# Pre-norm attention with a low-rank expert layer: two tiles first in the prologue, some tiles normalised on GpSimd, the layer's bias on TensorE

## The chip, the cores and the metric

The kernel runs on one core of one Trainium2 chip. The metric is the device time of one execution in microseconds (us). Engines by the names of the profile: PE is TensorE (PEld its weight loads), DVE VectorE, ACT ScalarE, POOL GpSimd, SP SyncE, which here only issues DMAs; SPq and ACTq are the queues of DMA-issuing instructions.

## The reference

x is 8 x 256 x 128 in float32. First attention over 16 heads of 64 is added to x, then a linear layer with eight low-rank experts.

```python
x = x + attention(layernorm(x))
x = x + ffn(layernorm(x))
# attention, for each batch and head:
scores = q @ k.T * 64**-0.5 + einsum('id,ijd->ij', q, rel_k[clip(i - j, -64, 64) + 64])
scores = where(scores < 32nd largest of the row, -inf, scores)
attn = softmax(scores)
a1 = attn @ v + einsum('ij,ijd->id', attn, rel_v[...]); a2 = attn @ a1; a3 = attn @ a2
out = (al0 * a1 + al1 * a2 + al2 * a3) @ Wout.T + bout
# ffn:
y = x @ base_w.T + base_b
gate = softmax(x @ router_w.T + router_b)            # 8 experts
y = y + 2 * sum over e of gate[e] * (x @ lora_A) @ lora_B[e]
```

## The kernel before

x lies as 16 tiles of 128 rows, two (T = 2) for each batch. The heads are worked off in pairs: 8 batches by 8 pairs (NP) are 64 pairs, 128 heads g. Each engine runs its own list of instructions, and semaphores tie them. The lists are written as slots q = -3 to 67, a software pipeline over the pairs: in slot q TensorE makes queries and keys of pair q+3 (`queries_and_keys`), the product with the relative keys of pair q+2 (`relative_keys`) and the scores of pair q+1 (`scores`); VectorE finds the top 32 of heads 2q and 2q+1 (`top`, four rounds of MAX8 with MATCH_REPLACE8 between them); ScalarE and GpSimd turn them into the softmax one head behind.

The relative term needs a shift of each row by its number. ScalarE copies the product out (`save_band`), GpSimd fills its edges (`fill_band`), SyncE writes it to a scratch in HBM (band_scratch) and reads it back at a slant (skew), and GpSimd adds it to the scores (`add_skew`, which releases `top`). The scratch has zeros written to it once.

For head g the way from the top values to the softmax is: `scale_limit` (GpSimd, after the last MAX8 of g), `ramp` (ScalarE, "pen"), `add_penalty` (GpSimd), `exponent` (ScalarE), and the reciprocal of its sum on VectorE in `divide(g)`, which stands at the end of `top(g+1)`. So an exponent that comes late holds VectorE there.

SyncE's order in the prologue is: x and the weights `wqkv`, the zeros of the scratch, eight small loads, then the slots; after slot -1 `load_wout` (wout, bout and the zeros of a second scratch, diag_scratch), after slot 0 `load_ffn`. `wqkv` has one block of 192 KB for each of the eight pairs of a batch. Its parts have semaphores: w_in for blocks 0 and 1, w_in2 for 2 to 7. TensorE waits for w_in2 in `queries_and_keys(2)`, ahead of slot 0.

The second norm and the layer (`layer`, 144 columns: 128 of the layer, 8 of the router, 8 of lora_A) run in the loop for the first six batches (INSIDE), one batch in eight slots, and save to ffn without bias. In the tail VectorE adds the bias to 12 tiles (`add_bias`, twice six), and GpSimd adds ffn onto the residual (`add_base`), whose tile is named x_sb in the profile. Four pairs' outputs are mixed on VectorE in the tail (`mix_part`) and projected on TensorE (`project_mix`).

Of the kernel before, what the change touches and what calls it, by code (L numbers as in the profile page):

```python
# [6 lines left out]
def preln_attention_ffn(nc: bass.Bass, x_d, wqkv_d, bqkv_d, wout_d, bout_d, relk_d, relv_d, relvc_d, alphas_d,  # L7
# [43 lines left out]
    with ctx:  # L51
# [1254 lines left out]
```

## Time and profile before

| | us |
|---|---|
| median of 3 runs (lowest, highest) | 702.81 (702.47, 704.76) |
| the profiled execution, its own time | 702.51 |
| its span in the profile | 700.8 |
| VectorE busy | 682.2 (97%) |
| TensorE busy | 651.9 (93%) |
| ScalarE busy | 619.5 (88%) |
| GpSimd busy | 549.4 (78%) |
| share of the chain that ended last: VectorE, TensorE, GpSimd | 76%, 11%, 3% |

The profiled execution lies 0.30 us under the median, inside the spread of the runs. Span and own time differ by 1.7 us, which lie around the profiled instructions. The busy shares are means over three stages: a prologue up to the first MAX8, a loop of 128 heads, and a tail behind the last one.

### The profile page before, as it was taken

The numbers are of one execution on the slowest core, as the hardware profiler recorded it, in microseconds if no ns is written. First come the engines' busy times: TensorE is split into PE (matmuls) and PEld (weight loads), VectorE is DVE, ScalarE is ACT, GpSimd is POOL, SyncE is SP. The second block draws the span as 40 slices with busy tenths as digits, with TensorE's granted clock in tenths as the row PEclk, the third lists the DMA queues.
The fourth block names the chain that finished last, engine by engine and source line by source line (L and its number), as shares of the span: only waits on it lengthen the run. The fifth ranks groups of instructions, "written<-read, shape, count | busy, mean of one in ns | idle before, by whom it ended". The sixth has DMA issues, their size and how long they took to land.

```text
span 700.8 us, 20904 instructions
## 1 busy us (share of the span) xinstructions
PE 651.9 (93%) x5748; PEld 505.8 (72%) x5748; DVE 682.2 (97%) x2827; ACT 619.5 (88%) x1772; POOL 549.4 (78%) x985
## 2 busy tenths in 40 slices
PE   5388999999999999999999999999999999998896
PEld 3266777777777777777787777877777777777664
DVE  6899999999999999999999999999999999999995
ACT  4589998999999999999999999998999999998763
POOL 1589898888878888878887888788887888877760
PEclk9789999999999999999999999999999999999998
DMA  6854454545455544545454545444454545445322
GB/s 200 184 146 146 140 153 127 164 131 161 125 154 140 154 136 135 152 130 167 131 159 126 153 139 145 147 151 140 131 154 135 164 133 154 129 130 162 87 58 61
DMA packets 148338, 98.72 MB, mean 141 GB/s; under 512 B 10624, under 2 KB 147968, under 8 KB 148096
## 3 DMA queue, kind: packets, MB, share of 16 engines
q1 hardware_dynamic: 147920, 97.32, 48.1%
q8 instruction: 48, 0.79, 0.5%
q14 instruction: 66, 0.54, 0.3%
q10 hardware_dynamic: 304, 0.08, 0.1%
HBM read 45.59 MB, written 51.77 MB: 139 GB/s over the span
## 4 chain that ended last, share of the span: by engine, by line
DVE 76%; PE 11%; issue 5%; POOL 3%; DMA 2%; ACT 2%; DVEq 1%; SPq 1%; ACTq 0%; POOLq 0%
DVE top L790 37%; DVE work L796 36%; PE ps_p L1053 2%; DMA band_scratch<-zeros 1%; PE ps_y L1073 1%; DVE rinv L777 1%; POOL s_sb L347 1%; PE ps_a L961 1%; PE ps_s L1010 1%; ACT a_sb L505 1%; PE ps_d L1030 1%; POOL a_sb L352 1%; PE ps_p L999 1%; DVEq L185 1%; POOL s_sb L322 1%
## 5 line engine op out<-in xcount | busy, mean ns | idle before, releaser
L790 DVE MAX8 top<-work 128x8 f32<-128x256 f32 x768 | 286.0, 415 | 0.0
L796 DVE MATCH_REPLACE8 work<-top,work 128x256 f32<-128x256 f32 x512 | 205.9, 410 | 0.0
L347 POOL TENSOR_TENSOR s_sb<-s_sb,pen 128x512 f32<-128x512 f32 x127 | 162.0, 1275 | 25.6 <-ACT pen L495 20.1
L505 ACT ACTIVATE a_sb<-s_sb,nmax 128x256 f32<-128x256 f32 x254 | 127.3, 502 | 23.1 <-POOL s_sb L347 14.6
L322 POOL TENSOR_TENSOR s_sb<-s_sb,skew 128x384 f32<-128x384 f32 x128 | 128.3, 1003 | 2.9 <-DMA skew<-band_scratch 2.9
L495 ACT ACTIVATE pen<-s_sb,limit 128x256 f32<-128x256 f32 x254 | 116.4, 512 | 12.6 <-POOL limit L334 12.3
L1053 PE MATMUL ps_p<-aT,rows 128*64 128x256 f32 x1024 | 125.3, 386 | 1.8 <-ACT rows L585 1.0
L352 POOL TENSOR_SCALAR a_sb<-a_sb,rinv 128x256 f32<-128x256 f32 x254 | 118.8, 478 | 1.6 <-DVE rinv L777 1.5
L796 DVE MATCH_REPLACE8 work<-top,s_sb 128x256 f32<-128x256 f32 x256 | 102.9, 410 | 0.0
L1053 PEld LDWEIGHTS ps_p<-aT,rows 128*64 128x64 f32 x1024 | 67.6, 136 | 40.5 <-issue 10.4
L790 DVE MAX8 top<-s_sb 128x8 f32<-128x256 f32 x256 | 94.1, 410 | 2.1 <-POOL s_sb L322 2.1
L961 PE MATMUL ps_a<-ident,a_sb 128*128 128x128 f32 x512 | 84.8, 289 | 12.2 <-POOL a_sb L352 12.2
L334 POOL TENSOR_SCALAR limit<-top 128x2 f32<-128x2 f32 x127 | 24.3, 192 | 81.0 <-DVE top L790 80.7
L961 PEld LDWEIGHTS ps_a<-ident,a_sb 128*128 128x128 f32 x512 | 54.5, 142 | 43.5 <-issue 28.8
L488 ACT COPY aT<-ps_a 128x512 f32<-128x512 f32 x128 | 72.3, 565 | 1.2 <-PE ps_a L961 1.2
L543 ACT COPY s_sb<-ps_s 128x512 f32<-128x512 f32 x128 | 68.9, 595 | 0.3 <-PE ps_s L1010 0.2
L1030 PE MATMUL ps_d<-aT,v_sb 128*64 128x256 f32 x504 | 65.4, 381 | 2.5 <-ACT diagT L548 2.5
L1010 PE MATMUL ps_s<-k_sb,q_sb 64*128 64x256 f32 x512 | 66.2, 377 | 0.0
L975 PE MATMUL ps_qk<-xnT,wqkv 128*128 128x256 f32 x128 | 43.8, 425 | 10.2 <-ACT v_sb L553 8.2
L1030 PEld LDWEIGHTS ps_d<-aT,v_sb 128*64 128x64 f32 x504 | 35.4, 137 | 21.8 <-ACT diagT L548 4.7
L999 PEld LDWEIGHTS ps_p<-relkt,q_sb 64*128 64x128 f32 x512 | 34.2, 190 | 22.7 <-issue 22.7
L361 POOL TENSOR_TENSOR clip<-aT,mask 128x256 f32<-128x256 f32 x64 | 47.9, 748 | 3.3 <-ACT aT L488 3.3
(176 smaller groups left out, 1331.8 us busy)
## 6 DMA issues: line engine op xcount, KB each, us to landing
skew<-band_scratch SPq DMA_DIRECT2D x128, 192.0 KB, 2.8
diag_scratch<-a_sb SPq DMA_DIRECT2D x128, 192.0 KB, 3.1
band_scratch<-band SPq DMA_DIRECT2D x128, 191.0 KB, 3.7
diag<-diag_scratch SPq DMA_DIRECT2D x128, 128.0 KB, 2.2
wqkv<-in_wqkv SPq DMA_DIRECT2D x1, 1152.0 KB, 8.0
x_sb<-in_x SPq DMA_DIRECT2D x4, 256.0 KB, 4.9
wout<-in_wout SPq DMA_DIRECT2D x1, 512.0 KB, 6.1
out<-xn SPq DMA_DIRECT2D x1, 512.0 KB, 3.2
```

The source lines that it names most:

```text
L322: nc.gpsimd.tensor_tensor(near, near, skew[p % 2][:, g % 2, :, :], ALU.add).then_inc(s_added, 1)
L347: nc.gpsimd.tensor_tensor(s_sb[g % 4][:], s_sb[g % 4][:], pen[g % 2][:], ALU.subtract).then_inc(pen_added, 1)
L352: nc.gpsimd.tensor_scalar(a_sb[g % 3][:, t, :], a_sb[g % 3][:, t, :], rinv[g % 2][:, t:t + 1], 1.0, ALU.mult, ALU.mult).then_inc(normed, 1)
L488: nc.scalar.copy(aT[p % 4][:, g % 2, :, :].rearrange("p c n -> p (c n)"), ps_a[:]).then_inc(t_saved, 1)
L495: nc.scalar.activation(pen[g % 2][:, t, :], s_sb[g % 4][:, t, :], ACT.Relu, bias=limit[g % 2][:, t:t + 1], scale=-STEEP).then_inc(ramp_don ...
L505: nc.scalar.activation(a_sb[g % 3][:, t, :], s_sb[g % 4][:, t, :], ACT.Exp, bias=nmax[g % 2][:, t:t + 1], scale=1.0, accum_out=rsum[g % 2] ...
L790: nc.vector.max(m[:, t, 8 * n:8 * n + 8], src).then_inc(top_step, 1)
L796: nc.vector.match_replace(work[t][:, n % 2, :], m[:, t, 8 * n:8 * n + 8], src, LOW).then_inc(top_step, 1)
L961: last = transpose(ps_a[:, c * N + t * P:c * N + (t + 1) * P], a_sb[g % 3][:, t, c * P:(c + 1) * P], ident[:])
L1010: last = mm(ps_s[h][:, t * N:(t + 1) * N], q_sb[p % 3][d, t * P:(t + 1) * P], k_sb[p % 3][d, :], start=True, stop=True)
L1030: mm(r1[d, 0:N], v_sb[p % 2][:, c, d], aT[p % 4][:, h, c, :], start=(c == 0), stop=False)
L1053: last = mm(ps[d, 0:N], r[:, i, c, d], aT[p % 4][:, h, c, :], start=(c == 0), stop=(c == T - 1))
```

## The change

In the prologue two tiles of x (one batch) and one block of weights come first, then the zeros, then the rest of x, and the eight small loads are one (`late`, laid out on the host). The remaining weights go in three parts: block 1 (w_in), blocks 2 and 3 (w_in2), issued inside slot -1, and blocks 4 to 7 (w_in3), issued after slot -1. TensorE multiplies `ones` by itself 11 times (WARM) before it has work. VectorE takes the moments and the norm of two tiles first; of the other 14 it normalises 8, GpSimd 6 (tiles 10 to 13 in slot -1, 14 and 15 in slot 0). The columns of xn go to TensorE in five groups (2, 4, 4, 4, 2 tiles) in place of four. ScalarE takes the second root after the copies of pairs 0 and 1. In the loop `layer` begins with a product of the identity and the bias, and GpSimd's `add_base` runs for two tiles at the end of slots 19, 27, ... 59. In the tail VectorE's two `add_bias` and GpSimd's two additions over six tiles are gone.

```diff
 @block.sync
-            for g in range(GROUPS):
-                sp.dma_start(x_sb[:, 4 * g:4 * g + 4, :], x_d[2 * g:2 * g + 2].rearrange("b (t p) d -> p (b t) d", p=P)
-                             ).then_inc(x_in[g], 16)
-                if g == 0:
-                    sp.dma_start(wqkv[:, 0:2, :], wqkv_d[:, 0:2 * 3 * P].rearrange("p (h c) -> p h c", h=2)).then_inc(w_in, 16)
-            sp.dma_start(wqkv[:, 2:NP, :], wqkv_d[:, 2 * 3 * P:].rearrange("p (h c) -> p h c", h=NP - 2)).then_inc(w_in2, 16)
-            sp.wait_ge(made, MADE)
+            load_x(0, 1, x_first)
+            load_weights(0, 1, w_first)
+            sp.wait_ge(made, 2)
             for i in range(2):
                 dst = bass.AP(band_d[i].tensor, DYN, [[2 * ROW, P], [ROW, 2], [1, P]])
                 sp.dma_start(dst, zeros[:, 0:2 * P].rearrange("p (h c) -> p h c", h=2)).then_inc(scratch_zero, 16)
-            for dst, src in ((relvc[0:DH, :], relvc_d), (relvc[DH:P, :], relvc_d),
...
-                sp.dma_start(dst, src).then_inc(late_in, 16)
+            load_x(1, 2, x_in[0])
+            load_weights(1, 2, w_in)
+            for g in range(1, GROUPS):
+                load_x(2 * g, 2 * g + 2, x_in[g])
+            sp.dma_start(late[:], late_d).then_inc(late_in, 16)
...
+                if q == -1:
+                    load_weights(2, 4, w_in2)
...
                 if q == -1:
+                    load_weights(4, NP, w_in3)
                     load_wout()
 @block.gpsimd
+            def normal_rows(a, e):
+                pool.wait_ge(rstd_done, 2)
+                for i in range(a, e):
+                    nc.gpsimd.tensor_scalar(xn[:, i, :], x_sb[:, i, :], mv[:, i, 0:1], rstd[:, i:i + 1], ALU.subtract,
+                                            ALU.mult).then_inc(xn_aside, 1)
...
+                if b >= 1 and q % NP == 3:
+                    pool.wait_ge(layer_saved, T * b)
+                    add_base(T * (b - 1), T * b)
...
-            for i, (a, e) in enumerate(((0, T * INSIDE // 2), (T * INSIDE // 2, T * INSIDE), (T * INSIDE, DONE))):
-                pool.wait_ge(f_saved, i + 1)
-                add_base(a, e)
+            pool.wait_ge(f_saved, 1)
+            add_base(T * INSIDE, DONE)
 @block.scalar
             save_queries(0)
+            save_band(0)
+            save_scores(0)
+            save_queries(1)
+            save_band(1)
             act.wait_ge(var_done, 2)
-            nc.scalar.activation(std[:, 4:TILES], mv[:, 4:TILES, 1], ACT.Sqrt).then_inc(std_done, 1)
-            save_band(0)
+            nc.scalar.activation(std[:, T:TILES], mv[:, T:TILES, 1], ACT.Sqrt).then_inc(std_done, 1)
             act.wait_ge(made, MADE)
             nc.scalar.activation(warm[:, 0:1], warm[:, 0:1], ACT.Exp).then_inc(warmed, 1)
-            save_queries(1)
-            save_band(1)
-            save_scores(0)
-            act.wait_ge(late_in, 16 * 8)
+            act.wait_ge(late_in, 16)
 @block.vector
-            moments(0, 4)
+            moments(0, T)
             dve.wait_ge(std_done, 1)
-            normal_rows(0, 4)
+            normal_rows(1, 0, T, T)
...
-            add_bias(0, T * INSIDE // 2)
-            add_bias(T * INSIDE // 2, T * INSIDE)
+            dve.wait_ge(layer_saved, T * INSIDE)
             add_layer_bias(T * INSIDE, DONE)
 @block.tensor
-                mm(ps_p1[:, N:N + FFN], ynT[:, i * P:(i + 1) * P], wffn[:], start=True, stop=True).then_inc(layer_ready, 1)
+                mm(ps_p1[:, N:N + FFN], ident[:], bffn[:], start=True, stop=False)
+                mm(ps_p1[:, N:N + FFN], ynT[:, i * P:(i + 1) * P], wffn[:], start=False, stop=True).then_inc(layer_ready, 1)
...
+            pe.wait_ge(made, 2)
+            for _ in range(WARM):
+                mm(ps_d[:, 0:P], ones[:], ones[:], start=True, stop=True)
             pe.wait_ge(made, MADE)
             normal_columns(0)
             queries_and_keys(0)
-            for q in (-2, -1):
-                relative_keys(q + 2)
-                if on(q + 1):
-                    scores(q + 1)
-                queries_and_keys(q + 3)
+            relative_keys(0)
+            scores(0)
+            queries_and_keys(1)
+            relative_keys(1)
+            queries_and_keys(2)
```


SyncE's order, from the first write of the scratch to the reads of pair 1 (band is the write of the scratch, skew the read; the waits name semaphores). Before:

```order
L280 DMA band_scratch<-band 128x2x191 [waits band_filled,scratch_zero]
L280 DMA band_scratch<-band 128x2x191 [waits band_filled]
L264 DMA skew<-band_scratch 128x2x192 [waits band_out0]
L264 DMA skew<-band_scratch 128x2x192 [waits band_out1]
L280 DMA band_scratch<-band 128x2x191 [waits band_filled] x2
L230 DMA wout<-in_wout 128x8x128
L230 DMA bout<-in_bout 128x128
L233 DMA diag_scratch<-zeros 128x2x64 x4
L264 DMA skew<-band_scratch 128x2x192 [waits band_out2]
L264 DMA skew<-band_scratch 128x2x192 [waits band_out3]
```

And now:

```order
L289 DMA band_scratch<-band 128x2x191 [waits band_filled,scratch_zero]
L289 DMA band_scratch<-band 128x2x191 [waits band_filled]
L271 DMA skew<-band_scratch 128x2x192 [waits band_out0]
L271 DMA skew<-band_scratch 128x2x192 [waits band_out1]
L219 DMA wqkv<-in_wqkv 128x768
L289 DMA band_scratch<-band 128x2x191 [waits band_filled] x2
L219 DMA wqkv<-in_wqkv 128x1536
L237 DMA wout<-in_wout 128x8x128
L237 DMA bout<-in_bout 128x128
L240 DMA diag_scratch<-zeros 128x2x64 x4
L271 DMA skew<-band_scratch 128x2x192 [waits band_out2]
L271 DMA skew<-band_scratch 128x2x192 [waits band_out3]
```

Weights of blocks 2 and 3 (128x768) and of 4 to 7 (128x1536) moved from ahead of the zeros, above this piece, to behind the first reads of the scratch, the first ahead of the write for pair 1, the second behind it.

TensorE's order from the relative keys of pair 1 to those of pair 2 (L975 and L978, now L1000 and L1003, are queries and keys; L999, now L1024, the relative keys; L1010 the scores). Before:

```order
L999 MATMUL ps_p<-relkt,q_sb 128x128 [waits band_saved,qk_saved,relk_done]
L999 MATMUL ps_p<-relkt,q_sb 128x128 x3
L1010 MATMUL ps_s<-k_sb,q_sb 128x256 [waits qk_saved]
L1010 MATMUL ps_s<-k_sb,q_sb 128x256 x3
L975 MATMUL ps_qk<-xnT,wqkv 128x256 [waits qk_saved,w_in2,xnT_saved]
L978 MATMUL ps_qk<-xnT,wqkv 128x256
L975 MATMUL ps_qk<-xnT,wqkv 128x256 [waits qk_saved,xnT_saved,relv_done]
L978 MATMUL ps_qk<-xnT,wqkv 128x256
L999 MATMUL ps_p<-relkt,q_sb 128x128 [waits band_saved,qk_saved,relk_done]
L999 MATMUL ps_p<-relkt,q_sb 128x128 x3
```

And now:

```order
L1024 MATMUL ps_p<-relkt,q_sb 128x128 [waits band_saved,qk_saved,relk_done]
L1024 MATMUL ps_p<-relkt,q_sb 128x128 x3
L1000 MATMUL ps_qk<-xnT,wqkv 128x256 [waits qk_saved,w_in2,xnT_saved]
L1003 MATMUL ps_qk<-xnT,wqkv 128x256
L1000 MATMUL ps_qk<-xnT,wqkv 128x256 [waits qk_saved,xnT_saved,relv_done]
L1003 MATMUL ps_qk<-xnT,wqkv 128x256
L1024 MATMUL ps_p<-relkt,q_sb 128x128 [waits band_saved,qk_saved,relk_done]
L1024 MATMUL ps_p<-relkt,q_sb 128x128 x3
```

The scores of pair 0, which stood behind the relative keys of pair 1, moved ahead of the queries of pair 1; the wait on w_in2 stands where it did, between pair 1 and all that follows.

GpSimd's order around the first heads (L332 is `add_skew`, L337 the norm, L343 `negative_max`, L359 `fill_band`, L350 `scale_limit`, L363 `add_penalty`), now:

```order
L337 TENSOR_SCALAR xn<-x_sb,mv,rstd 128x128 [waits rstd_done]
L337 TENSOR_SCALAR xn<-x_sb,mv,rstd 128x128 x3
L332 TENSOR_TENSOR s_sb<-s_sb,skew 128x2x192 [waits s_saved,skew_in0]
L343 TENSOR_SCALAR nmax<-top_0 128x2 [waits top_step]
L332 TENSOR_TENSOR s_sb<-s_sb,skew 128x2x192 [waits s_saved,skew_in1]
L337 TENSOR_SCALAR xn<-x_sb,mv,rstd 128x128 [waits rstd_done]
L337 TENSOR_SCALAR xn<-x_sb,mv,rstd 128x128
L359 TENSOR_SCALAR band<-band 128x2x2x63 [waits band_saved]
L350 TENSOR_SCALAR limit<-top_0 128x2 [waits top_step]
L343 TENSOR_SCALAR nmax<-top_1 128x2 [waits top_step]
L363 TENSOR_TENSOR s_sb<-s_sb,pen 128x512 [waits ramp_done]
L332 TENSOR_TENSOR s_sb<-s_sb,skew 128x2x192 [waits s_saved,skew_in2]
```

The two stretches of L337 are new, and the fill of pair 2's band stood ahead of the second `add_skew` before.

## Rows read from the trace of the kernel before

**Rows 1.** Windows of the prologue, the loop and the tail: busy us and instructions of each engine.

```profile
20.10:671.00 650.90, 619.69 (x5515) 483.42 (x5512) 649.56 (x2716) 597.61 (x1722) 537.69 (x961) 0.99 0.50 143
```

**Rows 2.** Chain that ended last, in order of time: start us, us, what.

```profile
4.63 9.11 DMA band_scratch<-zeros
...
13.76 2.77 DMA band_scratch<-band
...
20.14 0.74 DVE top L790 x2
...
30.25 0.64 DVE top L790 x2
```

**Rows 3.** Timeline of the prologue: start us, us, engine, line, op, tiles, count.

```profile
0.92 0.53 POOL L301 MEMSET zeros<- 128x512 f32 x1
...
7.08 1.09 PE L953 MATMUL ps_y<-ident,xn 128*128 128x128 f32 x4 [7.08 <-DVE xn L752]
...
8.84 1.22 PE L975 MATMUL ps_qk<-xnT,wqkv 128*128 128x256 f32 x2 [0.67 <-ACT xnT L482]
...
10.85 1.23 PE L999 MATMUL ps_p<-relkt,q_sb 64*128 64x128 f32 x8
...
12.92 0.44 POOL L343 TENSOR_SCALAR band<-band 128x252 f32<-128x252 f32 x1 [9.79 <-ACT band L537]
...
19.42 0.72 PE L999 MATMUL ps_p<-relkt,q_sb 64*128 64x128 f32 x8
...
19.97 1.03 PE L1010 MATMUL ps_s<-k_sb,q_sb 64*128 64x256 f32 x8
```

**Rows 4.** Timeline of TensorE from 39 us on.

```profile
39.08 1.10 PE L975 MATMUL ps_qk<-xnT,wqkv 128*128 128x256 f32 x2
39.98 1.06 PE L978 MATMUL ps_qk<-xnT,wqkv 128*128 128x256 f32 x2
```

**Rows 5.** Windows of TensorE after 27 us: busy us, granted clock, DMA share, GB/s.

```profile
27.00:28.00 1.00, 0.00 (x0) 0.86 1.11 367
28.00:29.00 1.00, 0.00 (x0) 0.50 1.08 315
```

**Rows 6.** Windows of the prologue, all engines: the last figure is GB/s.

```profile
9.00:10.00 1.00, 1.00 (x3) 0.82 (x4) 1.00 (x9) 0.00 (x0) 0.00 (x0) 1.00 0.98 404
```

**Rows 7.** Timeline of SyncE, 18 to 19 us.

```profile
18.09 0.36 SPq L264 DMA_DIRECT2D skew<-band_scratch  x1
18.49 0.47 SPq L280 DMA_DIRECT2D band_scratch<-band  x1
```

**Rows 8.** DMA issues: KB each, median us to landing.

```profile
wqkv<-in_wqkv SPq DMA_DIRECT2D x1, 384.0 KB, 4.1
```

**Rows 9.** Timeline, 21 to 29 us, ScalarE and GpSimd.

```profile
21.03 1.07 ACT L543 COPY s_sb<-ps_s 128x512 f32<-128x512 f32 x2
...
25.52 0.91 ACT L495 ACTIVATE pen<-s_sb,limit 128x256 f32<-128x256 f32 x2 [3.42 <-POOL limit L334]
...
28.18 1.00 POOL L322 TENSOR_TENSOR s_sb<-s_sb,skew 128x384 f32<-128x384 f32 x1 [0.40 <-DMA skew<-band_scratch]
...
28.72 0.19 ACT L505 ACTIVATION_READ_ACCUMULATOR a_sb<-s_sb,nmax 128x1 f32 x1
```

**Rows 10.** Timeline of the tail.

```profile
674.27 1.92 DVE L836 TENSOR_TENSOR ffn<-ffn,bffn 128x816 f32<-128x816 f32 x2
...
676.74 4.36 POOL L443 TENSOR_TENSOR x_sb<-x_sb,ffn 128x768 f32<-128x768 f32 x3
...
676.89 1.79 DVE L848 TENSOR_TENSOR gate<-ffn,lmax 128x112 f32<-128x112 f32 x1
...
681.96 0.71 PE L1081 MATMUL ps_y<-wout,mix 128*128 128x128 f32 x4 [0.43 <-DVE mix L864]
```

**Rows 11.** Timeline of GpSimd in slot 27.

```profile
303.70 0.19 POOL L334 TENSOR_SCALAR limit<-top 128x2 f32<-128x2 f32 x1 [1.40 <-DVE top L790]
```

**Rows 12.** Groups of GpSimd's instructions: count, busy us, mean ns.

```profile
L410 POOL TENSOR_TENSOR x_sb<-x_sb,yp_sb 128x256 f32<-128x256 f32 x7 | 5.1, 730 | 0.0
```

More of the change, by code:

```diff
@@ L31, in preln_attention_ffn @@
     T = N // P
+    ORDER = (late_d.shape[1] - T - 2 * T * DH) // NP
     TILES = B * T
@@ L203, in preln_attention_ffn @@
         DONE = TILES - T
+        WARM = 11
+        ASIDE = DONE - 4
         GROUPS = TILES // 4
+        COLUMNS = [(0, T)] + [(a, min(a + 4, TILES)) for a in range(T, TILES, 4)]
         MIXED = PAIRS - len(mix)
@@ L747, in moments, with normal_rows @@
                 nc.vector.tensor_scalar(mv[:, a:e, 1], mv[:, a:e, 1], EPS, None, ALU.add).then_inc(var_done, 1)
[L749 to L751 removed]
+            def normal_rows(n, a, e, last):
+                nc.vector.reciprocal(rstd[:, a:e], std[:, a:e]).then_inc(rstd_done, 1)
+                dve.wait_ge(rstd_done, n)
+                for i in range(a, last):
                     nc.vector.tensor_scalar(xn[:, i, :], x_sb[:, i, :], mv[:, i, 0:1], rstd[:, i:i + 1],
                                             ALU.subtract, ALU.mult).then_inc(xn_done, 1)
[L755 removed]
+            moments(0, T)
             dve.wait_ge(std_done, 1)
[L757 to L758 removed]
+            normal_rows(1, 0, T, T)
+            dve.wait_ge(relk_in, 16)
             own(nc.vector.tensor_scalar(relkt[:, 0, :], relk[:, 0:P], relk[:, P:VOCAB], None, ALU.subtract))
@@ L890, in _ @@
             dve.wait_ge(alpha_exp, 1)
-            own(nc.vector.tensor_scalar(al[:], al[:], 1.0, None, ALU.add))
-            nc.vector.reciprocal(al[:], al[:]).then_inc(alpha_done, 1)
+            own(nc.vector.tensor_scalar(al, al, 1.0, None, ALU.add))
+            nc.vector.reciprocal(al, al).then_inc(alpha_done, 1)
             for g in range(HEADS):
@@ L949, in normal_columns @@
             def normal_columns(g):
-                pe.wait_ge(xn_done, 4 * (g + 1))
+                a, e = COLUMNS[g]
+                if e <= ASIDE:
+                    pe.wait_ge(xn_done, e)
+                else:
+                    pe.wait_ge(xn_aside, e - ASIDE)
                 reach(pe, xnT_saved, g)
-                for i in range(4):
-                    last = transpose(ps_y[:, i * P:(i + 1) * P], xn[:, 4 * g + i, :], ident[:])
+                for i in range(a, e):
+                    last = transpose(ps_y[:, (i - a) * P:(i - a + 1) * P], xn[:, i, :], ident[:])
                 last.then_inc(xnT_ready, 1)
```

94 lines of the change are left out of this document (49 added, 45 removed).

## The prediction

> **What bounds the kernel now.** I read the windows by stage first. From 20.1 to 671 us VectorE works 649.56 of 650.90 us [rows 1]: the loop is its own bound, and 1.3 us is all that any rearrangement inside it could win. So the change can pay at two places, before the loop and behind it, and only by what reaches VectorE. The chain in order of time shows the first: the zeros of the scratch land at 13.74 us, pair 0's band is written (issued 13.76), read back and added, and the first MAX8 runs at 20.14 us; 10.11 us later, at 30.25 us, head 2 begins [rows 2]. From the issue of the band to the first MAX8 it is 6.38 us. In the prologue's timeline TensorE starts at 7.08 us and the band's edges are filled by 12.92 + 0.44 = 13.36 us [rows 3], 0.4 us before the zeros have landed. So before, two chains end together there: the zeros, queued behind all weights, and the computation.
>
> **The early prologue.** TensorE's first products are slow: queries 1.22 us and relative keys 1.23 us, where the same shape takes 0.72 us at 19.42 us [rows 3]. The windows show the clock go from 0.86 to 0.50 of the full 2.4 GHz by 28 us, after TensorE had been idle since 24 us [rows 5], and with 0.50 granted the queries take 1.10 us [rows 4]; so I read the prologue's first products as running at 1.2 GHz too. The products of ones can start when GpSimd's zeros are made, 0.92 + 0.53 = 1.45 us [rows 3]. One of 256 columns follows another by 39.98 - 39.08 = 0.90 us at the low clock [rows 4], so one of 128 by 0.45 us, and 11 end at 6.4 us, a little earlier if the clock rises among them; I take 6.2 us. Two normalised tiles are there before that (my estimate is 5.4 us), so TensorE begins 0.9 us earlier than before, and at the high clock. From 7.08 to 13.36 us lie 6.28 us. Half the transposes at twice the rate save 0.7 of 1.09 us, the queries 0.6 of 1.22, the relative keys 0.51 of 1.23 [rows 3], a copy of half the columns some 0.2: 2.0 us. The band is filled at 6.2 + 6.28 - 2.0 = 10.5 us and issued at once, since the zeros now have less data ahead of them; if the clock stays low, it is 11.5 us. The first MAX8 comes at 10.5 + 6.4 = 16.9 us, 3.2 us earlier.
>
> On the Trainium skill's page "SBUF — State Buffer", section "Who interferes with whom", VectorE and GpSimd share a port pair that one holds for a whole instruction. By that rule the 8 norms of VectorE and the 4 of GpSimd in slot -1 would stand in each other's way, and top(0) would come at some 17.3 in place of 16.9 us. The trace agrees in the tail, where a VectorE instruction over 112 elements takes 1.79 us beside GpSimd's long addition [rows 10]. As the next part has it, neither figure is the one that counts.
>
> **What is late next.** Head 2 can't begin before its skewed scores are added and before VectorE has passed `divide(0)` at the end of top(1), which needs exponent(0). Both get later relative to the start.
>
> Weights of blocks 2 and 3 are issued behind the read of pair 0's second head, and that read waits for its own write: before, it was issued at 18.09 us [rows 7], 4.33 us after the band. The next issue stood at 18.49 us [rows 7], 4.73 us after the band. So they are issued at 10.5 + 4.7 = 15.2 us. 384 KB took 4.1 us to land behind x [rows 8]; with less ahead I take 3.2 us, the ends being 2.8 and 4.1: landed at 18.4 us (18.0 to 19.3). Up to then TensorE can do nothing behind the relative keys of pair 1, which end near 12.3 us. That is 6 us of idleness; before, 4 us sufficed for the clock to drop [rows 5]. I therefore cost what follows at the low clock: queries and keys of pair 2 to 18.4 + 1.96 (39.08 to 41.04) [rows 4], the keys' copy and its wait 0.65, pair 3's queries and keys 1.8, relative keys of pair 2 1.16, and scores twice the 1.03 us of [rows 3] less their overlap, 1.9: 7.5 us. The last copy of the scores adds 0.6 (a half of 1.07) [rows 9]: 26.5 us. Only then does ScalarE come to ramp(0), since it stands behind these copies. From ramp to the end of exponent it took 25.52 to 28.91, 3.4 us [rows 9], and the reciprocal 0.2: head 2 begins at 18.4 + 11.7 = 30.1 us against 30.25 us. Before, ScalarE had done the scores by 22.10 us and waited 3.42 us for the limit [rows 9]; that reserve pays for the shift. **The 3.2 us won at head 0 come down to 0.15 us at head 2.**
>
> The page "TensorE: Matmul & The Clock Gate", section "Part 1: The HAM clock gate", of the Trainium skill says that the throttled clock is the default and only activity lifts it. By that rule the 11 products of ones buy speed for the first pair and lose it again in this wait.
>
> **The other limit of head 2** is the DMA queue. Before, from the issue of pair 1's band at 18.49 us [rows 7] to the landing of its skew at 28.18 us [rows 9] it was 9.7 us with the DMA engines nearly full, its share over 1 near the end [rows 5]. Now this begins at 15.7 us and has 1152 KB of weights in it, which at 404 GB/s [rows 6] are 2.9 us: landed at 28.3 us, or 27.8 us if some fill the gaps; plus 1.0 us of addition [rows 9], head 2 at 28.8 to 29.3 us. At the high clock this one decides, otherwise the 30.1 us.
>
> **The loop.** 12 products of 144 columns are added on TensorE, some 0.25 us each, far from the heads that VectorE needs next: nothing. GpSimd gets six additions of 128x256 at 0.73 us (L410 is the same shape) [rows 12], at a slot's end, where in slot 27 it waited 1.40 us for the next limit [rows 11]: hidden. Behind them stand `scale_limit` and the softmax chain; without that cover each costs 0.73 us, 4.4 us together. The six norms on GpSimd (estimate: under 0.5 us each) stand ahead of additions that have a whole head's time.
>
> **The tail.** VectorE loses 1.92 us of bias additions, GpSimd most of its 4.36 us, beside which VectorE's 1.79 us would shrink to some 0.3 [rows 10]. VectorE gains over 4 us there. But it is not the bound: TensorE waited 0.43 us for the mix at 681.96 us [rows 10], and otherwise works through its own chain of powers with ScalarE, to which the last residual is tied. Gain 0.45 us; floor 0, and if the mixes had been on the path throughout, 2 us.
>
> **Sum.** 0.15 + 0.45 = 0.6 us off the profiled execution's 702.51 us: 701.9 us. That execution lies 0.3 us below the median of the runs, 702.81 us, from which it would be 702.2 us. Since the errors I know of (clock, packing of DMAs) mostly shorten, I put it at 701.8 us.
>
> **Rivals.**
> 1. *The queue decides* (the clock is up when the weights land, or rises soon): head 2 at 28.8 to 29.3, so 0.95 to 1.45 plus 0.45: 700.6 to 701.1 us. For it: the idle stretch is cut short if the weights land early. Against it: idleness beyond that of [rows 5].
> 2. *The whole gain arrives:* VectorE runs through from 16.9, head 2 at 27.0, 3.25 + 0.45 = 3.7 us: 698.8 us. It wants weights by some 18 us, a high clock, and a queue 2 us faster than I cost it. For it: the zeros and small loads no longer delay anything.
> 3. *Slower: the second part of the weights.* Head 2 begins 11.7 us after they land. The edge is 19.0 us: with the tail's gain, landing later than that loses. At 20 us head 2 begins at 31.7: 1.45 lost, 0.45 won, 703.5 us; more than 0.3% slower takes a landing after 21.1 us, as would come with the band at 11.5 us and a landing time far over the 4.1 us of [rows 8].
>
> **How the numbers follow.** A measurement here tells about 0.3%, 2.1 us. Forecast 0.55 (its own range 700.6 to 703.1, from the ends of the landing and of the clock in the prologue), rival 1 0.2, rival 2 0.13, rival 3 0.12. Faster by over 2.1 us: all of rival 2, the lower end of rival 1 and a little of the forecast, 0.24. Slower: half of rival 3, 0.06. Same: 0.70. The range is 698.8 to 703.4 us: it takes in rival 2's value and half of rival 3.
>
> **What would show it.** Right: the first MAX8 near 17 us, TensorE idle from 12.3 to 18.4 us, its queries of pair 2 over 1 us long, VectorE waiting 2 to 3 us for exponent(0) or for the skew ahead of head 2, head 2 near 30 us; no new waits of VectorE in the loop; at the tail's mixes no wait of TensorE, and the last MAX8 to the end 0.45 us shorter. Wrong: no wait ahead of head 2 (rival 2), or a stall at slots 19 to 59, which would say that GpSimd's additions delay the limit.

## The result, and the profile of the changed kernel

Over 22 runs each in turn, the kernel before took 703.27 us (median; 700.91 to 705.97) and the changed one 704.65 us (702.48 to 708.74): a ratio of 1.0023 with a 95% interval of 1.0012 to 1.0033. The change costs 1.6 us by this ratio (1.4 us between the two medians). That is less than the 0.3% named in the prediction, but the interval excludes no change, and 704.65 us lies above the predicted range. The profiled execution took 706.07 us, its span 704.3 us (before 702.51 and 700.8).

The timeline of the prologue of the changed kernel, all engines:

```profile
1.51 5.06 PE L1217 MATMUL ps_d<-ones 128*128 128x128 f32 x22 [1.51 <-POOL zeros L311]
...
7.46 0.70 PE L1000 MATMUL ps_qk<-xnT,wqkv 128*128 128x256 f32 x2 [0.46 <-ACT xnT L506]
...
8.88 0.71 PE L1024 MATMUL ps_p<-relkt,q_sb 64*128 64x128 f32 x8 [0.29 <-ACT q_sb L549]
...
10.90 0.88 SPq L289 DMA_DIRECT2D band_scratch<-band  x2
...
14.28 3.28 POOL L337 TENSOR_SCALAR xn<-x_sb,mv,rstd 128x128 f32<-128x128 f32 x4
...
15.02 0.47 SPq L219 DMA_DIRECT2D wqkv<-in_wqkv  x1
...
17.53 0.99 POOL L332 TENSOR_TENSOR s_sb<-s_sb,skew 128x384 f32<-128x384 f32 x1
...
18.55 0.75 DVE L817 MAX8 top<-s_sb 128x8 f32<-128x256 f32 x2 [1.61 <-POOL s_sb L332]
...
20.50 1.19 PE L1000 MATMUL ps_qk<-xnT,wqkv 128*128 128x256 f32 x2 [7.65 <-issue]
...
28.18 1.07 ACT L567 COPY s_sb<-ps_s 128x512 f32<-128x512 f32 x2 [0.67 <-PE ps_s L1035]
...
29.14 0.92 ACT L519 ACTIVATE pen<-s_sb,limit 128x256 f32<-128x256 f32 x2
...
32.56 0.17 DVE L804 RECIPROCAL rinv<-rsum 128x2 f32<-128x2 f32 x1 [3.96 <-ACT a_sb L529]
32.67 0.75 DVE L817 MAX8 top<-s_sb 128x8 f32<-128x256 f32 x2
```

Read from the top: the products of ones end at 6.6 us, and the queries and relative keys of pair 0 take 0.70 and 0.71 us in place of the 1.22 and 1.23 of [rows 3]. Pair 0's band is issued at 10.90 us, 2.9 us earlier than in [rows 2]. At 18.55 the first MAX8 runs, 1.6 us earlier. But TensorE idles for 7.65 us until the weights of blocks 2 and 3 are there, ScalarE comes to the mask of head 0 (`pen`) only behind copies of scores that TensorE makes after that wait, and VectorE, done with head 1, waits 3.96 us. Its MAX8 at 32.67 us is head 2, which stood at 30.25 us in [rows 2]. The 1.6 us won at head 0 are 2.4 us lost at head 2.

The DMA issues of the weights, with KB and us from issue to landing, answer to [rows 8]:

```profile
wqkv<-in_wqkv SPq DMA_DIRECT2D x1, 768.0 KB, 7.8
...
wqkv<-in_wqkv SPq DMA_DIRECT2D x1, 384.0 KB, 5.4
```

15.02 + 5.4 = 20.4 us: the product at 20.50 us starts as they land. TensorE's windows (busy us, granted clock, DMA share, GB/s) show what the idle stretch does to the clock, as [rows 5] did before:

```profile
12.00:13.00 1.00, 0.72 (x8) 1.00 1.01 318
13.00:14.00 1.00, 0.00 (x0) 1.00 0.05 14
14.00:15.00 1.00, 0.00 (x0) 0.51 0.32 39
```

TensorE works 0.72 us in the first of these windows and then stands still; in the one from 14 us on the grant is 0.51, that is, it falls from 2.4 to 1.2 GHz, and the queries at 20.50 us take 1.19 us.

The window of the loop, from the MAX8 of head 2 to the last mask, has the columns of [rows 1]:

```profile
32.60:675.20 642.60, 617.57 (x5507) 483.08 (x5508) 640.36 (x2676) 594.70 (x1712) 537.72 (x958) 0.99 0.49 142
```

VectorE idles 2.2 us in it, 0.9 us more than before. Most of that are two waits, at 276.41 us (0.33) and 288.22 us (1.44), each 6 us behind a late diagonal on TensorE. One of these in the timeline:

```profile
270.69 0.63 PE L1046 MATMUL ps_d<-ident,diag 128*128 128x128 f32 x4 [1.67 <-issue]
...
276.41 0.17 DVE L804 RECIPROCAL rinv<-rsum 128x2 f32<-128x2 f32 x1 [0.33 <-ACT a_sb L529]
```

GpSimd's six additions, 0.73 to 0.74 us each, lie in slots where it waits for VectorE anyway. The tail, beside [rows 10]:

```profile
679.43 0.46 DVE L862 TENSOR_TENSOR ffn<-ps_s,bffn 128x288 f32<-128x288 f32 x1 [0.80 <-PE ps_s L1243]
...
680.18 0.73 POOL L428 TENSOR_TENSOR x_sb<-x_sb,ffn 128x256 f32<-128x256 f32 x1
680.23 0.82 DVE L868 TENSOR_TENSOR gate<-ffn,lmax 128x112 f32<-128x112 f32 x1
...
684.53 0.48 DVE L884 SCALAR_TENSOR_TENSOR mix<-r3T,late,mix 128x256 f32<-128x256 f32 x1 [2.70 <-ACT r3T L595]
```

The bias additions of 1.92 us are gone, GpSimd has one addition in place of three, and the gate takes 0.82 us in place of 1.79. VectorE now waits 2.70 us for ScalarE. From the last mask (670.73 us before, 675.01 after) to the start of VectorE's last addition it is 27.30 us before and 26.62 after: 0.68 us won.

**The books of the two profiles.** Head 2 +2.5 us (the timeline has before's at 30.16 us, from where the chain of [rows 2] follows on at 30.25), loop +1.8 us (from 640.6 to 642.3), tail -0.7 us: +3.6 us, against spans that differ by 3.5 us. All runs together give 1.6 us only, which is about head 2 and the tail alone (+1.8). So either the loop's 1.8 us belong to the profiled execution, or the profiles mislead. The experiments had to settle that, and what head 2 waits for.

### The profile page after: what moved, and what is told of

Read it like the earlier page. It is cut to its first block, busy times and chain, and to the rows that moved or that the text cites. A ratio compares the mean times of both kernels' runs of the same rounds, so it can differ in the third digit from the quotient of the medians.

```text
span 704.3 us, 20995 instructions
## 1 busy us (share of the span) xinstructions
PE 658.7 (94%) x5794; PEld 513.0 (73%) x5794; DVE 677.0 (96%) x2819; ACT 620.6 (88%) x1773; POOL 554.3 (79%) x995
## 4 chain that ended last, share of the span: by engine, by line
DVE 64%; PE 24%; issue 4%; POOL 2%; ACT 1%; DVEq 1%; ACTq 0%; POOLq 0%
DVE top L817 32%; DVE work L823 31%; PE ps_p L1078 5%; PE ps_y L1098 3%; PE ps_a L984 2%; PE ps_d L1055 2%; PE ps_s L1035 2%; PE ps_p L1024 1%; PE ps_qk L1000 1%; PE ps_d L1046 1%; PE ps_qk L1011 1%; PE ps_d L1063 1%; PE ps_d L1128 1%; PE ps_qk L1003 1%; POOL s_sb L363 1%
## 5 line engine op out<-in xcount | busy, mean ns | idle before, releaser
L363 POOL TENSOR_TENSOR s_sb<-s_sb,pen 128x512 f32<-128x512 f32 x127 | 161.9, 1275 | 35.3 <-ACT pen L519 30.7
L332 POOL TENSOR_TENSOR s_sb<-s_sb,skew 128x384 f32<-128x384 f32 x128 | 128.4, 1003 | 0.0
L984 PEld LDWEIGHTS ps_a<-ident,a_sb 128*128 128x128 f32 x512 | 54.1, 141 | 39.7 <-issue 28.8
L350 POOL TENSOR_SCALAR limit<-top 128x2 f32<-128x2 f32 x127 | 24.3, 191 | 66.2 <-DVE top L817 66.1
L1000 PE MATMUL ps_qk<-xnT,wqkv 128*128 128x256 f32 x128 | 42.9, 418 | 16.0 <-issue 7.7
L1024 PEld LDWEIGHTS ps_p<-relkt,q_sb 64*128 64x128 f32 x512 | 34.4, 190 | 22.7 <-issue 22.7
```

What stands on the lines that cost most here:

```text
L332: nc.gpsimd.tensor_tensor(near, near, skew[p % 2][:, g % 2, :, :], ALU.add).then_inc(s_added, 1)
L363: nc.gpsimd.tensor_tensor(s_sb[g % 4][:], s_sb[g % 4][:], pen[g % 2][:], ALU.subtract).then_inc(pen_added, 1)
L984: last = transpose(ps_a[:, c * N + t * P:c * N + (t + 1) * P], a_sb[g % 3][:, t, c * P:(c + 1) * P], ident[:])
```

## The experiments

All numbers of one kernel in one table. "Loop" is from head 2's first MAX8 to the last mask, "tail" from there to VectorE's last addition, in us, all from one profile; the ratio is to the kernel before in the same comparison. e1 to e4, e5 to e9, e10 to e13, and e14 with e15 were each compared on one chip; across these groups the ratios are less sure than within.

| kernel | first MAX8 | head 2 | loop | tail | ratio (95%) |
|---|---|---|---|---|---|
| before | 20.14 | 30.16 | 640.57 | 27.30 | 1 |
| changed | 18.55 | 32.67 | 642.34 | 26.62 | 1.0023 (1.0012 to 1.0033) |
| e1 loop and tail only | 20.62 | 30.64 | 640.91 | 26.76 | 0.9985 (0.9974 to 0.9996) |
| e2 prologue only | 18.59 | 32.13 | 641.52 | 27.31 | 1.0015 (1.0001 to 1.0029) |
| e3 weights early | 18.57 | 28.62 | 641.97 | 26.30 | 0.9981 (0.9968 to 0.9994) |
| e4 all weights early | 19.29 | 29.31 | 642.05 | 26.86 | 0.9984 (0.9970 to 0.9998) |
| e5 norms behind skew | 17.86 | 28.94 | 640.25 | 26.31 | 0.9986 (0.9972 to 0.9999) |
| e7 no ones | 18.89 | 28.91 | 639.97 | 26.76 | 0.9973 (0.9962 to 0.9984) |
| e8 one load | 18.81 | 34.94 | 640.56 | 26.32 | 1.0067 (1.0042 to 1.0092) |
| e9 wout later | 17.66 | 27.68 | 640.81 | 26.76 | 0.9976 (0.9964 to 0.9989) |
| e10 e9, no ones | 18.33 | 28.36 | 641.17 | 26.75 | 0.9948 (0.9927 to 0.9969) |
| e11 e9, norms on VectorE | 19.39 | 29.35 | 641.57 | 26.31 | 0.9969 (0.9948 to 0.9989) |
| e12 changed again | 18.39 | 32.84 | 640.83 | 26.75 | 1.0036 (1.0009 to 1.0063) |
| e13 before again | 19.89 | 29.92 | 642.42 | 27.33 | 0.9982 (0.9954 to 1.0010) |
| e14 weights alone | 18.47 | 31.96 | 643.12 | 26.63 | 1.0020 (1.0000 to 1.0041) |
| e15 blocks 4 to 7 later | 18.54 | 32.01 | 642.73 | 26.32 | 1.0005 (0.9984 to 1.0026) |

**The two halves of the change.** e1 has the prologue of before and the edits of loop and tail:

```diff
-                mm(ps_p1[:, N:N + FFN], ynT[...], wffn[:], start=True, stop=True).then_inc(layer_ready, 1)
+                mm(ps_p1[:, N:N + FFN], ident[:], bffn[:], start=True, stop=False)
+                mm(ps_p1[:, N:N + FFN], ynT[...], wffn[:], start=False, stop=True).then_inc(layer_ready, 1)
...
+                if b >= 1 and q % NP == 3:
+                    pool.wait_ge(layer_saved, T * b)
+                    add_base(T * (b - 1), T * b)
```

> The prologue of before with the change's loop and tail alone. Theory (the late weights of pairs 2 and 3 cost the time, the loop edits are hidden and the tail gains 0.7 us): 0.1% faster than before, about 702.6 us, head 2 near 30.2 us, no new wait of VectorE in the loop. Rival (the bias on TensorE or GpSimd's additions bring the stalls seen in the loop of the changed kernel, 1.8 us near 280 us): 0.1 to 0.3% slower than before, with waits of VectorE for the exponent between 200 and 660 us.

Measured: ratio 0.9985, 1.1 us faster, interval 0.3 to 1.8. In the loop VectorE waits twice, 0.3 us each, and the tail is 0.54 us shorter than before's. e2 is the reverse, the new prologue with loop and tail of before.

> The change's prologue with the loop and tail of before. Theory: slower than before by what head 2 is late (2.4 us in the profile) and a little more, 0.3 to 0.4%, about 705.5 us. Rival (the loop edits cost the time): equal to before or faster.

Measured: ratio 1.0015, 1.1 us slower; half of what was expected; VectorE waits 3.38 us ahead of head 2, at 32.13 us. So the loss is in the prologue, and the rest of the change is a gain. The size of each is less sure: the two halves add up to nothing, where the whole change costs 1.6 us, and the three intervals together allow for about 1.5 us. e1 also shows how far an unaltered prologue moves by itself: its head 2 comes at 30.64 us, in the two profiles of the kernel before at 30.16 and 29.92.

**What head 2 waits for.** e3 is the changed kernel with one line moved: blocks 2 and 3 are loaded behind `late` and no longer behind the skew read of pair 0.

```diff
             sp.dma_start(late[:], late_d).then_inc(late_in, 16)
+            load_weights(2, 4, w_in2)
...
-                if q == -1:
-                    load_weights(2, 4, w_in2)
```

> The changed kernel with the weights of pairs 2 and 3 issued right behind the load of the small tensors, ahead of the waits of the slots. Theory: TensorE's 7.7 us wait ahead of the queries of pair 2 goes, head 2 begins one run of top(0) and top(1) after the first MAX8, at 28.7 us in place of 32.7 us, and the time falls by 4 us to about 700.7 us, 0.35% under before. Rival (the DMA queue holds the skew of pair 1 anyway): head 2 at 30 us or later, 702 us.

The timeline of e3 (TensorE, SyncE, GpSimd, VectorE):

```profile
12.87 0.70 PE L999 MATMUL ps_qk<-xnT,wqkv 128*128 128x256 f32 x2
...
16.58 0.44 SPq L238 DMA_DIRECT2D wout<-in_wout  x1
...
18.16 5.10 SPq L241 DMA_DIRECT2D diag_scratch<-zeros  x4
...
23.30 0.98 SPq L272 DMA_DIRECT2D skew<-band_scratch  x2
...
27.59 1.00 POOL L331 TENSOR_TENSOR s_sb<-s_sb,skew 128x384 f32<-128x384 f32 x1 [1.38 <-DMA skew<-band_scratch]
...
28.62 0.76 DVE L816 MAX8 top<-s_sb 128x8 f32<-128x256 f32 x2
```

TensorE has pair 2's weights at 12.87 us, VectorE's wait of 3.96 us is gone, and head 2 begins at 28.62 us, 4.05 us earlier than in the changed kernel. The time is now below that of before (0.9981, where 0.35% less was expected). One line turns the loss into a gain. The row at 27.59 shows the next limit: the skew of pair 1 lands only 1 us ahead of head 2.

e4 loads blocks 4 to 7 there as well (`load_weights(4, NP, w_in3)` behind the line above).

> As e3_w2_early, and the weights of pairs 4 to 7 behind them, so all weights are ahead of pair 0's band in the queue. Theory: the band waits for 1152 KB more, nearly 3 us, the first MAX8 comes at 19.5 to 20.5 us, and the time is 702 us. Rival (what queues behind the band does the harm, not what stands ahead): as fast as e3_w2_early or faster, near 700.5 us.

The additional 768 KB delay the skew of pair 0 (first MAX8 19.29), head 2 comes at 29.31, and the time is that of e3 within the intervals, not the 702 us of the theory (median 700.92).

e8 goes the other way and doubles the suspected cost: blocks 2 to 7 in one load at the changed kernel's place.

```diff
                 if q == -1:
-                    load_weights(2, 4, w_in2)
+                    load_weights(2, NP, w_in2)
...
-                    load_weights(4, NP, w_in3)
```

> The changed kernel, with the weights of blocks 2 to 7 in one load at the place where it loads blocks 2 and 3 (issued near 15.0 us). A doubling of the suspected cost. Theory (head 2 begins 12.2 us after these weights have landed): 1152 KB took 8.0 us before, so they land near 23.0 us in place of 20.4 and head 2 begins near 35.2 in place of 32.7, time 2.5 us above the changed kernel (ratio to before about 1.006). Rival (what delays the changed kernel against e3 is something else, for instance the second skew read or the traffic as a whole): head 2 within 0.5 us of 32.7 and no change in time, ratio 1.002.

```profile
23.17 1.19 PE L997 MATMUL ps_qk<-xnT,wqkv 128*128 128x256 f32 x2 [10.91 <-issue]
...
34.83 0.17 DVE L803 RECIPROCAL rinv<-rsum 128x2 f32<-128x2 f32 x1 [5.96 <-ACT a_sb L528]
```

The weights land 2.7 us later than in the changed kernel, and head 2 begins 2.3 us later, 11.8 us behind them (12.2 in the changed kernel); the ratio is 1.0067 (six runs), 4.7 us over before. The theory's 35.2 us was met within 0.3 us. That head 2 follows the landing of these weights is shown in both directions, and so is that the time follows head 2, if not us for us: e3 moves head 2 by 4.05 us and the ratio by 0.42%, 3.0 us.

**Why the landing took 5.4 us.** e14 issues everything that stood behind the 384 KB (blocks 4 to 7, wout, bout, zeros) behind the skew read of pair 1; e15 moves blocks 4 to 7 alone.

```diff
                         sp.dma_start(skew[p % 2][:, h, :, :], src).then_inc(skew_in[(2 * p + h) % 4], 16)
+                if q == 0:
+                    load_weights(4, NP, w_in3)
+                    load_wout()
...
-                if q == -1:
-                    load_weights(4, NP, w_in3)
-                    load_wout()
```

> The changed kernel with all that it issues behind the weights of blocks 2 and 3 (768 KB of weights at 16.52 us, wout, bout, the zeros of the diagonals) issued behind the read of pair 1's skew instead. In the changed kernel the 384 KB issued at 15.02 us landed at 20.4, 5.4 us later; before the change they took 4.1. Theory A (what is issued behind them shares the DMA engines and delays them): landed in 3.2 to 4.1 us, near 18.2 to 19.1 us, first product of pair 2 there, head 2 11.8 to 12.2 us later at 30.2 to 31.2 us, time 1.5 to 2.4 us below the changed kernel (ratio to before 1.000). Rival B (the reads and writes of the bands ahead of and beside them delay them): still 5.0 to 5.6 us, landing at 20.2 or later, head 2 above 32 us, no change against the changed kernel.

> The changed kernel with only the 768 KB of weights of blocks 4 to 7 moved behind the read of pair 1's skew; wout's 512 KB follow blocks 2 and 3 directly. Theory A by volume (anything large behind them delays them): 5 us or more as in the changed kernel, head 2 near 32.5. Theory A2 (the weights of blocks 4 to 7 in particular): as in e14. Rival B: as the changed kernel in both.

The row of these weights in e14, first, and in a second block in e15:

```profile
wqkv<-in_wqkv SPq DMA_DIRECT2D x1, 384.0 KB, 4.2
```

```profile
wqkv<-in_wqkv SPq DMA_DIRECT2D x1, 384.0 KB, 5.2
```

With only pair 1's band issued closely behind them they take 4.2 us, with wout's 512 KB behind them too 5.2, and in three profiles of the changed prologue 5.4, 5.4 (e2) and 6.0 us (e12). That fits theory A, which would put some 1.2 us down to the large loads behind, and the bands' traffic alone doesn't give 5 us, against rival B. But it is one profile each, and the kernel before speaks against it. This is its order of issue, and then the row of its 384 KB in e1, which has the same prologue:

```profile
0.79 0.45 SPq L210 DMA_DIRECT2D x_sb<-in_x  x1
...
1.30 0.49 SPq L213 DMA_DIRECT2D wqkv<-in_wqkv  x1
...
1.84 1.52 SPq L210 DMA_DIRECT2D x_sb<-in_x  x3
...
3.40 0.51 SPq L214 DMA_DIRECT2D wqkv<-in_wqkv  x1
```

```profile
wqkv<-in_wqkv SPq DMA_DIRECT2D x1, 384.0 KB, 5.6
```

There the 384 KB (blocks 0 and 1) have 768 KB of x and 1152 KB of weights issued behind them within 2.1 us, more than in the changed kernel, and landed in 4.1 us in both profiles of before, but in 5.6 us in e1. So one and the same place gives landings 1.5 us apart, more than the 1.2 us in question, and how much the loads behind cost stays open. Head 2 moved by 0.7 us only, to 31.96 (expected 30.2 to 31.2), and e2, with the changed kernel's prologue, has it at 32.13. It came 12.5 us behind the landing; a part of that is the scores, which took 1.92 us there and 1.58 in the changed kernel's profile. The two ratios don't part from the changed kernel's, and these two profiles have the longest loops of all.

**The other waits of the prologue.** e5 is e3 with GpSimd's four norms put behind the addition of pair 0's skew.

```diff
-                if q == -1:
-                    normal_rows(ASIDE, DONE)
...
                 if on(q + 1):
                     add_skew(2 * q + 2)
+                if q == -1:
+                    normal_rows(ASIDE, DONE)
```

> The kernel of e3 (weights of blocks 2 and 3 issued early), with GpSimd's four norms of slot -1 put behind the addition of pair 0's skew. In e3 that addition started at 17.54 us, the moment the four norms were done (14.08 + 3.49), and the first MAX8 at 18.57. Theory A (the norms delay the first head, the DMA queue decides head 2): the addition starts when the skew has landed, near 16.3 us (issue 13.81 + 2.6), first MAX8 17.3, 1.2 us earlier; but head 2 stays at 28.6, since the skew of pair 1 lands at 27.5 and its addition takes 1.0, so VectorE waits about 1.2 us there and the time stays that of e3 (ratio to before 0.998). Rival B (head 2 follows head 0 by 10.05 us whatever the queue does): head 2 at 27.35, the time 1.2 us below e3. Rival C (norms weren't what the addition waited for): first MAX8 stays at 18.5.

```profile
16.83 1.00 POOL L331 TENSOR_TENSOR s_sb<-s_sb,skew 128x384 f32<-128x384 f32 x1 [3.29 <-DMA skew<-band_scratch]
...
17.82 3.13 POOL L336 TENSOR_SCALAR xn<-x_sb,mv,rstd 128x128 f32<-128x128 f32 x4
17.86 0.75 DVE L816 MAX8 top<-s_sb 128x8 f32<-128x256 f32 x2 [0.88 <-POOL s_sb L331]
...
28.94 0.75 DVE L816 MAX8 top<-s_sb 128x8 f32<-128x256 f32 x2 [0.97 <-POOL s_sb L331]
```

Theory A: the first MAX8 comes 0.7 us earlier (1.2 expected), head 2 stays at 28.9 and VectorE waits there for the skew. The norms did delay head 0, and at head 2 that was worth nothing. e9 then takes away that wait too: e5 with `load_wout()` moved behind pair 1's skew read, at the place shown for e14.

> The kernel of e5 with the loads of wout, bout and the zeros of the diagonals issued behind the read of pair 1's skew in place of ahead of it. In e3 these issues occupied SP from 16.58 to 23.26 us and the read followed at 23.30. Theory A (SP's order and the queue decide head 2 once the weights are early): the read is issued near 19 to 20 us, lands by 23 to 24, head 2 no longer waits for it and begins 10.05 us behind the first MAX8, at 27.4 us (e3 28.6), if pair 1's scores and exponent(0) are done; time 1.2 us below e3, near 700.2 on the scale of e3's comparison, ratio to before about 0.996. Rival B (head 2 then waits for ScalarE's exponent(0), or the loop gives the gain back later): head 2 at 28.5, or a stall of VectorE of over 1 us before 60 us; no change against e3.

```profile
19.25 1.16 SPq L272 DMA_DIRECT2D skew<-band_scratch  x2
...
26.22 1.00 POOL L332 TENSOR_TENSOR s_sb<-s_sb,skew 128x384 f32<-128x384 f32 x1
...
27.68 0.73 DVE L817 MAX8 top<-s_sb 128x8 f32<-128x256 f32 x2
```

The read is issued 4 us earlier than in e3, and head 2 begins at 27.68, 10.02 us behind the first MAX8: VectorE runs through. The ratio is 0.9976, where about 0.996 was expected; beside e5 on the same chip the medians are 700.19 and 700.97 us. So the 1.2 us at head 2 are clear in the profile, while the intervals of the two ratios overlap.

e7 is e3 with `WARM = 0`, without the products of ones.

> The kernel of e3 without the 11 products of ones. Theory (the products lift the clock for the first pair): the queries and relative keys of pair 0 take over 1.1 us in place of 0.70, the band of pair 0 is issued 0.9 to 1.5 us later than 10.99 us, at 11.9 to 12.5, and the first MAX8 moves by 0 to 0.6 us only, since GpSimd's norms end at 17.5 anyway; head 2 within 0.5 us of 28.6, time within 0.5 us of e3. Rival (they do nothing, the clock is granted anyway): durations 0.70 and the band issued within 0.2 us of 10.99. Rival 2 (the whole prologue moves with it): head 2 1 to 1.5 us later and the time 1 to 1.5 us above e3.

```profile
6.78 1.22 PE L999 MATMUL ps_qk<-xnT,wqkv 128*128 128x256 f32 x2 [0.46 <-ACT xnT L505]
...
10.81 0.70 PE L999 MATMUL ps_qk<-xnT,wqkv 128*128 128x256 f32 x2
...
11.34 0.89 SPq L288 DMA_DIRECT2D band_scratch<-band  x2
```

The first pair runs at the low level (1.22 us), but the product at 10.81 us has the duration of the high one (0.70). The band is issued 0.35 us later than in e3, below the 0.9 expected; head 2 is 0.3 us later, and the time isn't longer (700.01 us beside 700.97 of e5, and 700.19 of e9, though head 2 comes 1.2 us later than in e9). e10 is the same edit on e9, e11 is e9 with all norms on VectorE (`ASIDE = TILES`, no norms on GpSimd).

> The kernel of e9 without the products of ones. In e7 against e3 their absence made the band of pair 0 0.35 us later only, and head 2 0.3 us. Here the first MAX8 follows the landing of the skew directly, so theory A: band issued near 11.4 (e9 10.63), first MAX8 near 18.4 (17.66), head 2 near 28.4 (27.68), time 0.7 us above e9 (ratio to before 0.9985). Rival (the start of the prologue is hidden by what comes behind it, and a clock that stays up in the waits gives it back): head 2 within 0.3 us of 27.7 and no difference to e9.

> The kernel of e9 with all norms on VectorE, none on GpSimd. VectorE's 8 norms took 2.14 us in e9 (0.27 each), GpSimd's 0.79 each whether VectorE had norms or MAX8 beside them. Theory A (6 more norms are 1.6 us of VectorE ahead of its first MAX8): VectorE's norms end at 18.2 us in place of 16.5, its reciprocals at 18.7, first MAX8 18.7 in place of 17.66, head 2 28.7, time 1.0 us above e9. Rival (GpSimd's norms delay head 1 or the skew additions by as much): head 2 within 0.3 us of 27.7.

In e10 head 2 begins at 28.36, as theory A has it, but the time doesn't follow: its ratio is 0.9948, where 0.9985 was expected and e9, on another chip, had 0.9976. In e11 VectorE's 14 norms take 4.48 us; the first MAX8 comes at 19.39 (expected 18.7) and head 2 at 29.35 (28.7). What is missing stands in one row of the timeline of e11:

```profile
16.87 1.15 DVE L776 TENSOR_SCALAR xn<-x_sb,mv,rstd 128x128 f32<-128x128 f32 x1
16.94 0.99 POOL L332 TENSOR_TENSOR s_sb<-s_sb,skew 128x384 f32<-128x384 f32 x1 [2.84 <-DMA skew<-band_scratch]
```

This norm of VectorE took 1.15 us in place of 0.34 and ended 0.09 us behind GpSimd's addition. By head 2 the norms on GpSimd are worth 1.7 us, if they stand behind the skew's addition (29.35 for 27.68 in e9). In time that isn't shown: e11 wasn't run beside e9, and e10 (701.33 us, e11 702.75, before 704.09 on their chip) also lacks the ones. e9 and e10 weren't run side by side either, so which is the faster stays open; both are faster than before in their comparisons.

**Whose are the stalls in the loop?** e12 and e13 are the changed kernel and the one before, unaltered, profiled a second time.

> The changed kernel once more, unaltered, profiled again. In its first profile VectorE waited 0.33 and 1.44 us in the loop (276 and 288 us), and from head 2 to the last mask it took 642.3 us where before took 640.6. Theory A (these stalls belong to the run, not to the change): the prologue repeats (first MAX8 18.5, head 2 32 to 33), the stalls come at other places or not at all, head 2 to last mask anywhere in 640.0 to 642.3; the median stays 1.5 us above before. Rival B (GpSimd's additions or the bias products cause them): stalls of over 1 us again near 276 to 288 us and 642 us for the stretch.

> The kernel before, unaltered, profiled again, to see how far one profile's loop differs from another's. Theory A: first MAX8 and head 2 within 0.4 us of 20.1 and 30.2, head 2 to last mask in 640.0 to 642.3 us (640.6 in its first profile), with stalls at other places than before. Rival B (its loop is stall-free because it lacks the additions): 640.5 us again, no wait of VectorE over 0.5 us between 31 and 640 us. Time equal to before.

The timeline of e12, ahead of head 2 and near the loop's end, and of e13 in the loop:

```profile
32.72 0.17 DVE L804 RECIPROCAL rinv<-rsum 128x2 f32<-128x2 f32 x1 [4.28 <-ACT a_sb L529]
...
653.96 0.63 PE L1046 MATMUL ps_d<-ident,diag 128*128 128x128 f32 x4 [1.89 <-issue]
```

```profile
289.53 0.63 PE L1021 MATMUL ps_d<-ident,diag 128*128 128x128 f32 x4 [1.07 <-issue]
...
295.43 0.17 DVE L777 RECIPROCAL rinv<-rsum 128x2 f32<-128x2 f32 x1 [0.82 <-ACT a_sb L505]
```

The wait ahead of head 2 repeats (4.28 us). The stalls at 276 and 288 us don't; the loop is 640.83 us long in place of 642.34. And the kernel before, which has none of the additions, has such a stall at 295 us in its second profile and a loop of 642.42 us in place of 640.57. Theory A holds: a late diagonal on TensorE, and VectorE waiting 6 to 9 us later, belongs to a run, not to the change.

## Why the prediction was wrong

**The step that failed** is "384 KB took 4.1 us to land behind x [rows 8]; with less ahead I take 3.2 us, the ends being 2.8 and 4.1". They took 5.4 us (6.0 in e12). The issue at 15.02 us (forecast 15.2) held, and the rest of the sum nearly so: "Head 2 begins 11.7 us after they land" measured 12.2 us (11.8 in e8, 12.5 in e14). With a landing at 20.4 us the prediction's own formula gives 32.1 us for head 2, 1.9 us late, and with 0.7 us for the tail 1.2 us slower; the comparison measured 1.6. So rival 3 is what happened, near its line "At 20 us head 2 begins at 31.7". I gave it 0.12. The 3.2 us had no row behind it: no profile has 384 KB land in under 4.1 us. "Less ahead" wasn't so either: before, 256 KB of x went ahead of the load, here the two skew reads of 192 KB each. And [rows 8] was one landing in one profile, not an upper end; in e1 the same load took 5.6 us. Why it was 5.4 us here is known in part only. e14 and e15 point at the loads issued behind (4.2 and 5.2 us without all or some of them), but the 4.1 us of before had even more behind them.

**The first MAX8** was forecast at 16.9 us and came at 18.55. The band was issued at 10.90 (forecast 10.5); that is 0.4. The rest is GpSimd by the rows, since its addition starts at 17.53, as the fourth norm ends: I took its norms at "under 0.5 us each" and put them "ahead of additions that have a whole head's time". They took 0.79 to 0.86 us each, and the first four stand ahead of the addition for head 0, which has no such time. In e5, with the order changed, it came at 17.86, though the skew's read was issued 3.8 us behind the band there and 2.7 us in the changed kernel. For head 2 it didn't matter.

**The rule on the ports** (the Trainium skill, "SBUF — State Buffer", "Who interferes with whom") asked for norms on VectorE and GpSimd to stand in each other's way. Norm beside norm cost little: VectorE's 8 norms took 2.31 us beside GpSimd's and 2.14 in e9 where GpSimd had none beside them, and GpSimd's longest took 0.86 us in the changed kernel and 0.99 in e3, for 0.81 in e9. But the lines of e11 agree with the rule: there a norm of VectorE waited out GpSimd's whole addition, 1.15 us for 0.34. So do the 1.79 us of [rows 10], which are 0.82 us in the changed kernel, beside a GpSimd addition of 0.73 in place of 4.36 us.

**The clock.** The forecast that the ones lift it for the first pair (0.70 for 1.22 us) and that the wait for weights loses it again (1.19 us at 20.50) was right; the rule of the Trainium skill in "TensorE: Matmul & The Clock Gate", "Part 1: The HAM clock gate", that only activity lifts the clock, agrees with both rows. e7 adds that without the ones the work of the first pair lifts it too, for the second pair. In the prologue the level is read from these durations: the granted clock reads 1.00 from 9 to 10 us before the change [rows 6], where the queries still take 1.22 us.

**The other limit**, the queue at 28.8 to 29.3 us, was nearly right: with the weights early, VectorE waited 0.97 us for the skew in e5, with head 2 at 28.94 us; in e3 the skew's addition ended just as VectorE came to head 2, at 28.62. A part of it is SyncE's order of issue, which I hadn't seen: in e9 head 2 comes 1.2 us earlier by it. Rival 2, "VectorE runs through", is what e3, e4, e7 and e9 show once the weights are early, in e9 from 17.66 and not from 16.9.

**The loop** at nothing was right. GpSimd's additions took the forecast 0.73 us and no wait follows them; e1, with them and the old prologue, is faster than before. The waits that I named as a sign of the opposite ("new waits of VectorE in the loop") appear in the profile, and would have misled: the second profiles show them in the kernel before as well.

**The tail** was under-sized: 0.45 forecast, 0.44 to 1.0 in the profiles with its edits, 0.68 in the changed kernel. Its mechanism was right: TensorE's wait for the mix is gone, VectorE now waits 2.70 us for ScalarE, and the over 4 us saved on VectorE come to 0.7.

## What to carry to other kernels

Put the load that the engines wait for next ahead of everything that could be issued a microsecond later: here one line moved turned 1.6 us of loss into about 1.3 us of gain. Price a landing by several profiles and not by the one row at hand: 384 KB took anything from 4.1 to 6.6 us. Work that is made earlier at the start is worth what it brings at the first place where the bound engine runs through, so follow it two heads further before you count it. And before a stall of a microsecond in one profile is put down to an edit, profile both kernels twice.

## What the runs showed of the hardware

- A load of 384 KB took 4.1, 4.1 and 5.6 us to land in three profiles of one prologue (before, e13, e1), 5.4, 5.4 and 6.0 in three of another (changed, e2, e12), 4.2 in e14, 5.2 in e15, and 5.6 to 6.6 us in the seven in which it was issued at 6.4 to 6.6 us behind x and `late` (e3 to e7, e9 to e11).
- A VectorE norm of 128x128 that started 0.07 us ahead of a GpSimd addition of 128x384 ended only behind it, 1.15 us long in place of 0.34 (e11).
- A diagonal read that lands late holds TensorE for 0.8 to 2.4 us at places that differ in part from run to run of one kernel (115, 196 and 642 us in before's first profile, 196, 290 and 644 in its second; 271 and 282 us in the changed kernel's first, 128, 644 and 654 in its second). Near the loop's end, from 639 to 656 us, it comes in 14 of 16 profiles. In 16 profiles the loop was 640.0 to 643.1 us long. What makes the read late wasn't tried and stays open.
- GpSimd's norm of 128x128 by two columns of scalars took 0.79 to 0.99 us; VectorE's followed one another every 0.27 to 0.32 us.
